# The coupling net's turned products on VectorE alone, in another order, with the last tiles' output rows in the steps of the next attention

## What is computed

```python
def _L0_ffn_ref(x, ...):                       # x: layer-normed rows
    gf = _global_net(x.mean(axis=1, keepdims=True), ...)   # pooled net
    out = x
    for _ in range(3):
        tf = _coupling_net(out, ...)           # 256 -> 256 -> 128 -> 64 -> 1, gelu, sigmoid at the end
        coupling = 0.1 + adaptive_range * (0.7 * gf + 0.3 * tf - 0.5) * 2.0
        out = out + coupling * _twist(out)     # [p_r, -p_i, -o_r, o_i]
    return out
x = x + tanh(g_xattn[0]) * _L0_xattn_ref(layernorm(x), ctx_1024, ...)   # 16 heads of 64
x = x + tanh(g_ffn[0])   * _L0_ffn_ref(layernorm(x), ...)
x = x + tanh(g_xattn[1]) * _L1_xattn_ref(ctx_1024, layernorm(x), ...)   # 16 heads of 16
x = x + tanh(g_ffn[1])   * _L1_ffn_ref(layernorm(x), ...)               # shared expert and top 2 of 8 experts
```

## Time and profile before

| | us |
|---|---|
| median of 3 runs | 711.97 (711.93 to 715.17) |
| the profiled execution, its own time | 712.9 |
| its span, first to last instruction | 711.0 |
| TensorE busy (matmul) | 683.8 |
| VectorE busy | 397.5 |
| ScalarE busy | 287.0 |
| GpSimd busy | 181.0 |
[...]

### The profile page before, as it was taken

One profiled execution on the slowest core, in us unless ns is written; L12 is line 12 of the kernel. 1 busy time (PEld: TensorE's weight loads), 2 busy tenths in 40 slices (PEclk: granted clock), 3 DMA queues, 4 the chain that ended last, 5 costly groups with the idle time before them and its releaser, 6 DMA issues.

```text
span 711.0 us, 11363 instructions
## 1 busy us (share of the span) xinstructions
PE 683.8 (96%) x3640; PEld 475.8 (67%) x3641; DVE 397.5 (56%) x983; ACT 287.0 (40%) x609; POOL 181.0 (25%) x180
## 2 busy tenths in 40 slices
PE   7999999999999987989999999999999999999996
PEld 6777777777754344689999746656545777777765
DVE  4688887788634489478777658222332433333321
ACT  3555533453555653466777541111322222222220
POOL 3100000000002643376000103661123333333433
PEclk9999999999999988699999999999999999999998
DMA  9770000000000006003900201422662656666643
GB/s 291 199 257 16 1 0 0 0 0 0 1 0 8 2 1 222 16 1 128 346 0 1 89 1 38 141 91 80 203 190 56 153 147 179 175 169 164 164 98 36
DMA packets 54934, 65.16 MB, mean 92 GB/s; under 512 B 11582, under 2 KB 37904, under 8 KB 54894
## 3 DMA queue, kind: packets, MB, share of 16 engines
q1 hardware_dynamic: 47806, 55.31, 24.0%
q0 software_dynamic: 7088, 9.35, 7.6%
HBM read 48.48 MB, written 16.00 MB: 91 GB/s over the span
## 4 chain that ended last, share of the span: by engine, by line
PE 87%; issue 3%; DVE 3%; POOL 2%; ACT 2%; DMA 2%; POOLq 0%; SPq 0%; DVEq 0%; ACTq 0%
PE ps L619 78%; PE ps L622 10%; DMA early<-in_wq0T 1%; POOL x_rows L558 0%; POOL x_rows L557 0%; DVE work L2062 0%; POOL rstd L528 0%; ACT early L1479 0%; DVE early L2065 0%; POOL early L554 0%; DMA work<-expert_rows 0%; POOLq L137 0%; ACT work L1340 0%; POOL early L555 0%; ACT middle L1352 0%
## 5 line engine op out<-in xcount | busy, mean ns | idle before, releaser
L619 PE MATMUL ps<-middle,work 128*128 128x256 f32 (+4 forms) x656 | 177.4, 420 | 1.2 <-ACT work L1340 0.8
L1340 ACT ACTIVATE work<-ps 128x512 f32<-128x512 f32 (+3 forms) x209 | 83.0, 437 | 211.2 <-PE ps L622 195.4
L619 PEld LDWEIGHTS ps<-middle,work 128*128 128x128 f32 (+1 forms) x656 | 115.8, 183 | 48.2 <-issue 29.2
L619 PE MATMUL ps<-late,work 32*128 32x154 f32 (+6 forms) x912 | 145.2, 347 | 0.6 <-ACT work L1340 0.6
L585 POOL DMA_INDIRECT out_rows<-masks x47 | 70.4, 1497 | 153.2 <-DMA out_rows<-masks 66.2
L619 PEld LDWEIGHTS ps<-late,work 128*128 128x128 f32 (+3 forms) x912 | 95.3, 184 | 7.9 <-issue 4.7
L619 PE MATMUL ps<-work,late 128*128 128x256 f32 (+2 forms) x424 | 87.9, 367 | 0.6 <-ACT work L1340 0.5
L622 PE MATMUL ps<-consts_sb,work 128*128 128x128 f32 (+1 forms) x564 | 80.5, 277 | 6.1 <-DVE work L1804 3.2
L622 PEld LDWEIGHTS ps<-consts_sb,work 128*128 128x128 f32 (+1 forms) x564 | 65.3, 140 | 26.2 <-issue 11.1
L528 POOL TENSOR_TENSOR rstd<-var_eps,minus_half 128x8 f32<-128x8 f32 (+2 forms) x11 | 14.4, 1311 | 268.7 <-DVE var_eps L1816 268.7
L619 PEld LDWEIGHTS ps<-work,late 128*128 128x128 f32 (+1 forms) x424 | 72.6, 198 | 14.4 <-issue 4.8
(11 more groups left out here) (253 smaller groups left out, 801.7 us busy)
## 6 DMA issues: line engine op xcount, KB each, us to landing
late<-in_w SPq DMA_DIRECT2D x40, 512.0 KB, 4.3
early<-in_w SPq DMA_DIRECT2D x16, 512.0 KB, 10.6
expert_rows<-work SPq DMA_DIRECT2D x36, 130.0 KB, 2.7
work<-expert_rows SPq DMA_DIRECT2D x36, 130.0 KB, 2.2
middle<-in_w SPq DMA_DIRECT2D x8, 512.0 KB, 7.9
out_rows<-x_rows SPq DMA_DIRECT2D x4, 512.0 KB, 3.4
x_rows<-in_x SPq DMA_DIRECT2D x2, 768.0 KB, 10.6
late<-in_ws SPq DMA_DIRECT2D x3, 512.0 KB, 4.0
```

Of the source, the lines that this page charges most:

```text
L619: return nc.tensor.matmul(o, l, r, start=start, stop=stop, **kw)
L1340: return nc.scalar.activation(o, i, ACT.Copy)
```

## The change

- GpSimd loses `turn_z` and `out_rows_`; it keeps only the roots here. The semaphores `f_z1` and `f_row` go.
- VectorE gets `turn_z` of its own (four 512-column operations an item) after `turn_y(0)`, `turn_y(1)` and, for items 2 and 3, after `turn_y(5)`.
- For items 4 to 7 the multiply-add that forms c moves from VectorE to ScalarE: an Identity pass after the tanh in `act4`, behind a wait on that tanh.
- The pooled net's three products move forward, between the halves of `net1("y", 2)`. `to_columns(2)` moves ahead of `net2(1)`, `su1(1)` behind `to_columns(3)`. The order of `net1`, `net2`, `net3` and of their gelus changes, and the banks with it (`PRODUCT_BANK`).
- `couplings_by_row` multiplies by 32 columns of w4 (all alike) where it had one.
- On VectorE `xn0(0, 0)` and `xn0(0, 1)` come before the second pair of rows. The even pairs' rows (8) are spread up to step 1, the odd pairs' rows (8) over the steps 2 to 9, one a step, each with its statistics; `variances(8)` falls into step 6, `variances(9)` and the wait for its root between step 9 and the loop, which now begins at step 10.
- SP's experts' weights wait for `var_done` 10 instead of `f_row` 12.

```diff
-NORMS = [(0, 2), (2, 4), (4, 8), (0, 4), (4, 8), (0, 1), (1, 2), (2, 4), (4, 8), (0, 4), (4, 8)]
+NORMS = [(0, 2), (2, 4), (4, 8), (0, 4), (4, 8), (0, 1), (1, 2), (2, 4), (4, 6), (6, 8), (0, 4), (4, 8)]
+PRODUCT_BANK = {("y", 0): 0, ("y", 1): 4, ("y", 2): 0, ("z", 0): 4, ("y", 3): 0, ("z", 1): 4, ("z", 2): 0, ("z", 3): 4}
...
-            sp.wait_ge(q["f_row"], 12)
-            sp.wait_ge(q["var_done"], 7)
+            sp.wait_ge(q["var_done"], 10)
...
-                        at = 4 * (p // 2) + j
-                        last = mm(ps[:, 4 * k + p % 2, at:at + 1], h3[p][rows, P * j:P * j + P], fw4[rows, 0:1])
+                        at = 32 * (4 * (p // 2) + j)
+                        last = mm(ps[:, 4 * k + p % 2, at:at + 32], h3[p][rows, P * j:P * j + P], fw4[rows, 0:32])
...
             net1("y", 1)
             net2(0)
+            pe.wait_ge(q["f_cp"], evicted("y", 0))
+            to_columns(2, (0, 1))
             pe.wait_ge(q["n_res"], T)
             net2(1)
-            su1(1)
-            pe.wait_ge(q["f_cp"], evicted("y", 0))
-            to_columns(2, (0, 1))
             pe.wait_ge(q["f_cp"], evicted("y", 1))
             to_columns(3, (4, 5))
+            su1(1)
             net3(0)
...
+            net1("y", 2, (0,))
+            pooled([gwt2[:]], [gh1[:]], ps[0:64, 6, 0:B], 1)
+            net1("y", 2, (1,))
+            pooled([gwt3[:]], [gh2[:]], ps[:, 6, 0:B], 2)
+            net4(0)
             net1("z", 0)
-            net4(0)
-            pooled([gwt2[:]], [gh1[:]], ps[0:64, 6, 0:B], 1)
-            net1("z", 1)
-            pooled([gwt3[:]], [gh2[:]], ps[:, 6, 0:B], 2)
-            net1("y", 2)
             net1("y", 3)
             net2(2)
+            net1("z", 1)
             pe.wait_ge(q["f_gact"], 3)
             net2(3)
+            net2(4)
             net1("z", 2)
             net3(1)
-            net2(4)
+            net2(5)
             net4(1)
-            net2(5)
             net1("z", 3)
             net3(2)
             net4(2)
             couplings_by_row(0)
+            net2(6)
             couplings_by_row(1)
-            net2(6)
             net2(7)
             couplings_by_row(2)
             net3(3)
             net2(8)
             net4(3)
             net2(9)
+            net3(4)
             couplings_by_row(3)
-            net3(4)
             couplings_by_row(4)
...
             def act4(n):
 
                 act.wait_ge(q["f_l4"], n + 1)
-                nc.scalar.activation(tt[n], ps[:, 7 - 4 * (n % 2), :], ACT.Tanh, bias=hb[:, 1:2],
-                                     scale=0.5).then_inc(q["f_tanh"], 1)
+                last = nc.scalar.activation(tt[n], ps[:, 7 - 4 * (n % 2), :], ACT.Tanh, bias=hb[:, 1:2], scale=0.5)
+                if n >= NG:
+                    last.then_inc(q["f_t4"], 1)
+                    act.wait_ge(q["f_cpl"], 1)
+                    act.wait_ge(q["f_t4"], n - NG + 1)
+                    last = nc.scalar.activation(tt[n], tt[n], ACT.Identity, bias=cpl[:, 1 + n % 2:2 + n % 2],
+                                                scale=cpl[:, 0:1])
+                last.then_inc(q["f_tanh"], 1)
...
             act1s(8)
-            act1s(9)
             act2(8)
             act4(6)
             act4(7)
+            act1s(9)
             act2(9)
+            act3(4)
             by_row(1, 0, 2)
-            act3(4)
+            by_row(0, 2, 3)
             act1s(10)
-            by_row(0, 2, 3)
             act1s(11)
...
+            def turn_z(n):
+
+                g, c = ffn_group(n), tt[n]
+                seq.sync()
+                at = seq.n
+                for o in range(2):
+                    seq.mark(v.tensor_tensor(dve_u[2 + o], c, ys[:, g, o, :], ALU.mult))
+                for o in range(2):
+                    dve.wait_ge(q["dve_seq"], seq.base + at + o + 1)
+                    seq.mark(v.tensor_tensor(zs[:, g, o, :], zs[:, g, o, :], dve_u[2 + o], ALU.subtract))
...
-            for n in range(6):
+            def out_two(pi, j):
+
+                for k in range(2):
+                    out_row(pi, k, j)
+                seq.sync()
+                for k in range(2):
+                    norm_stats(4 * pi + j + TB * k)
+
+            turn_y(0)
+            turn_z(0)
+            turn_y(1)
+            turn_z(1)
+            for n in range(2, 6):
                 turn_y(n)
+            turn_z(2)
+            turn_z(3)
             two_cycles(0)
             turn_y(6)
             turn_y(7)
...
             xn0(0, 0, "a")
             xn0(0, 1, "a")
+            out_two(0, 1)
+            variances(6)
+            two_cycles(1)
             soft(0, 0, "a")
             dve.wait_ge(q["rstd_done"], 7)
             xn0(0, 2, "a")
+            out_two(0, 2)
             soft(0, 1, "a")
             xn0(0, 3, "a")
+            out_two(0, 3)
+            variances(7)
             three_cycles(1)
...
-            def step1_out(n, a, z):
+            def step1_out(n):
 
                 att1(0, n - 2)
+                if n == 6:
+                    variances(8)
                 soft(0, n, "a")
                 res1(0, n - 2)
+                if n == 6:
+                    dve.wait_ge(q["rstd_done"], 9)
                 xn0(0, n + 2, "a")
-                norm_stats(tile_of(0, n - 2))
-                row_stats(a, z)
...
+                norm_stats(tile_of(n // 2 - 1, n % 2))
+                out_row(1, n % 2, n // 2 - 1)
+                seq.sync()
+                norm_stats(TB // 2 + n // 2 - 1 + TB * (n % 2))
+
+            for n in range(2, 10):
+                step1_out(n)
+            variances(9)
+            dve.wait_ge(q["rstd_done"], 10)
+            with dve.Fori(5, TB - 1) as i:
```

More of the change, by code:

```diff
@@ L207, in build @@
         ys = cut(middle, 0, [NG, 2, G4]); zs = cut(middle, 4096, [NG, 2, G4])
-        dve_u = [cut(work, 1536 + 512 * o, [G4]) for o in range(2)]; pool_u = [cut(work, 2560 + 512 * o, [G4]) for o in range(2)]
-        wz = cut(masks, 1600, [KD, 256]); pool_r = cut(early, 14336, [2, D])
+        dve_u = [cut(work, 1536 + 512 * o, [G4]) for o in range(4)]
+        wz = cut(masks, 1600, [KD, 256])
         turn_t, turn_c = [cut(masks, 2112 + 48 * n, [2, 3, 2, 4]) for n in range(2)]
@@ L818, in to_columns, with net1 @@
                     last.then_inc(q["f_tx"], 1)
-            def net1(kind, n):
+            def net1(kind, n, os=range(2)):
                 g = ffn_group(n)
                 pe.wait_ge(q["f_cp"], max(evicted("x", n), PRODUCT_FREE[kind, n]))
-                for o in range(2):
+                for o in os:
                     for m in range(KD):
-                        last = mm(ps[:, 4 * (n % 2) + o, :], (fw1 if kind == "y" else wz)[:, m, P * o:P * o + P],
+                        last = mm(ps[:, PRODUCT_BANK[kind, n] + o, :], (fw1 if kind == "y" else wz)[:, m, P * o:P * o + P],
                                   st_x[:, m, g, :], m == 0, m == KD - 1)
@@ L1494, in act1, with first @@
                                      bias=par[:, V_CB1 + o:V_CB1 + o + 1]).then_inc(q["f_a1"], 1)
-            def first(n):
-                for o in range(2):
+            def first(n, os=range(2)):
+                for o in os:
                     act1(n, o)
-                    last = copy(ys[:, ffn_group(n), o, :], ps[:, 4 * (n % 2) + o, :])
-                last.then_inc(q["f_cp"], 1)
+                    last = copy(ys[:, ffn_group(n), o, :], ps[:, PRODUCT_BANK["y", n] + o, :])
+                if os[-1] == 1:
+                    last.then_inc(q["f_cp"], 1)
             def second(n):
@@ L1506, in second @@
                     act.wait_ge(q["f_l1"], product("z", n, o))
-                    last = copy(zs[:, ffn_group(n), o, :], ps[:, 4 * (n % 2) + o, :])
+                    last = copy(zs[:, ffn_group(n), o, :], ps[:, PRODUCT_BANK["z", n] + o, :])
                 last.then_inc(q["f_cp"], 1)
@@ L1552, in _ @@
             nc.scalar.activation(gh1[:], ps[:, 6, 0:B], ACT.Gelu, bias=par[:, V_GB1:V_GB1 + 1]).then_inc(q["f_gact"], 1)
-            second(0)
-            act4(0)
-            act4(1)
+            first(2, (0,))
             act.wait_ge(q["f_gmm"], 2)
@@ L1558, in _ @@
                                  bias=par[0:64, V_GB2:V_GB2 + 1]).then_inc(q["f_gact"], 1)
-            second(1)
+            first(2, (1,))
             act.wait_ge(q["f_gmm"], 3)
             nc.scalar.activation(gtan[:], ps[:, 6, 0:B], ACT.Tanh, bias=hb[:, 0:1], scale=0.5).then_inc(q["f_gact"], 1)
-            first(2)
+            act4(0)
+            act4(1)
+            second(0)
             first(3)
             act2(2)
+            act1s(4)
+            second(1)
             act2(3)
-            act1s(4)
+            act1s(5)
             second(2)
-            act1s(5)
             act3(1)
             act2(4)
+            act2(5)
             act4(2)
             act4(3)
-            act2(5)
             second(3)
@@ L2158, in _ @@
             xn0(0, 2, "a")
+            out_two(0, 2)
             soft(0, 1, "a")
```

(18 more changed lines are left out.)

104 lines of the change are left out of this document (17 added, 87 removed).

## The result

The median went from 711.95 to 723.98 us (four runs, 720.23 to 725.24); the ratio is 1.0162, with a 95% interval of 1.0137 to 1.0186. The forecast was 716.3 with an upper end of 720.5: the sign was right, the size was not. The profiled execution of after took 725.24 with a span of 723.4; before it was 712.9 and 711.0.

A forecast was written before the change was run, and what follows sets the result against it. TensorE was taken as the bound, 87% of the chain. First att1 at 303.2, plus 8.75, 49.9, 0.25 and 1.75, put step 10's att1 at 363.9, +4.3 us; added to the 711.97 median: 716.3 us, range 709.0 to 720.5.

The forecast's parts named there:

- Couplings of 32 columns: Row couplings on TensorE, net part: 1.25 us per group of 16 instructions, bounds 1.07 and 1.48.
- Clock at 250 to 257 cured: Wider coupling columns should cure TensorE's clock fall, where eight matmuls had taken 6.73 us instead of 3.6.
- Turned products on VectorE off the path: VectorE's turn_y and turn_z, about 2.5 us each, ready before ScalarE asks: cost 0, cover over 4 us.
- The new wait: TensorE ahead of net2(9): 3.6 us dry until ScalarE's act1s(9), now behind act2(8) and two tanh with passes.
- The clock behind it: Clock fall behind the 3.6 us gap, up to TensorE ready for the second attention: 1.7 us, between 0 and 3.4.
- Rival 3: Slower still: clock down from 262 until the second attention, couplings at 1.48, rows at 1.35: 721 us; chance 0.12.
- R to S 4.8, S to A 15.1: TensorE ready for second attention (R) to first soft (S) 4.8 us; from there to first att1 (A) 15.1.
- Steps 3 to 8 at 7.13, and 0.25 for `variances(8)`: Second-attention steps carrying a row: 7.13 us each, as work behind res1 adds in full; 0.25 for variances(8), bounds 0 and 0.6.
- Rival 1: Steps stay bound by TensorE, rows fall into VectorE's spare time: 6.45 us a step, 710.8 us; chance 0.16.
- Step 2 at 8.75: Second attention's step 2: 6.03 us up to res1 and 2.7 behind it, 8.75 against 8.0 before.
- The exposed root 1.75 us: Between the steps and the loop: variances(9) and the wait for its root add 1.75 us.
- E: The att1 of step 10, after which both kernels have the same instructions: 363.9 against 359.61, +4.3 us.

The follow-up runs named there:

- a2: The changed kernel with four 512-column dummy products filling TensorE's wait between net4(3) and net2(9): 717.04 us, ratio 1.0087 to the kernel before.
- e1: a1 with VectorE's eight rows ahead of res1, two in step 2 and one each in steps 3 to 8, variances(9) in step 9: 706.92 us.
- d1: The changed kernel with the row of steps 2 to 9 ahead of res1, its statistics still behind: 718.82 us, ratio 1.0098 to the kernel before.
- c4: c3 with three more dummy matmuls in step 2, between its scores and its transposes: 701.96 us, ratio 0.9863 to the kernel before.
- c3: The changed kernel with act1s(9) before act2(8), odd pairs' rows on GpSimd, two dummy matmuls each before net2(8) and behind net2(9): 704.14 us.
- a1: The changed kernel with act1s(9) on ScalarE moved back ahead of act2(8): 715.95 us, ratio 1.0056 to the kernel before.
- a5: The changed kernel with the multiply-add of items 4 to 7 back on VectorE instead of ScalarE's added passes: 720.10 us, ratio 1.0107 to before.

## Why the prediction was wrong in size, by its steps

1. *Pooled net*: -0.66 forecast; `act3` started at 245.62, 1.2 us earlier than before. Right, a little short.
2. *Couplings of 32 columns*: 1.25 us a group (1.07 to 1.48) forecast, 0.98 to 1.08 measured. So 32 columns cost here what one did, 1.08 against the 1.07 of the earlier trace rows. Taking the price of a column from a row that mixes shapes was the error. It did not show in the sum: from `act3` to the end of `net3(3)` it took 10.27 us, where 10.26 was forecast, since a wait of 0.65 us for ScalarE that the walk did not have took its place.
3. *Clock at 250 to 257 cured*: right, 1.00 against 0.54.
4. *Turned products on VectorE off the path*: right. Alone it did pairs in 1.29 us, and no TensorE wait at R ended with it.
5. *The new wait*: 3.6 us ended by ScalarE forecast, 4.39 measured. The new pass took 0.81 us, not 0.66, so the two tanh with their passes took 2.98 us and not 2.7, and the first tanh started only as `net4(3)` ended, not 0.4 us before. At full clock the late start behind it costs 3.4 us (a2 against e1).
6. *The clock behind it*: this is the step that failed. I put 1.7 us on it, bounds 0 and 3.4, from the 4 us at 0.57 of the earlier trace rows. It was 7.4 (after against a2): 6.4 behind the new wait, and 1.0 that arose ahead of it, where the clock fell behind the wait of 2.01 us (0.60 at 258 to 262); in the kernel before it had held behind the same wait (1.00 at 261 to 265). The nearest row for a clock behind a wait over 3 us was the other one in the same group: 3.19 us of wait, then 12.4 us at 0.50, of which TensorE worked 11.31 and so lost up to 5.7. I named it as the likeness and then priced from the other. Even that would have been a guess, as 1.4, 5.1 and 6.4 us behind the same wait show; the bound of 3.4 was the error more than the 1.7. Rival 3, the slower one with the clock down to R, was the right mechanism; it had the same wrong price.
7. *R to S 4.8, S to A 15.1*: 3.62 and 14.73 measured. A row was 1.05 us rather than 1.19. These gave back 1.6 us.
8. *Steps 3 to 8 at 7.13, and 0.25 for `variances(8)`*: 7.18 on average, which is the forecast. In these steps what stands behind `res1` adds in full; d1 shows it by taking the row from there (6.52 for 7.11). Rival 1, steps bound by TensorE at 6.45, is refuted for rows in that place, and close (6.52) for rows ahead of `res1`.
9. *Step 2 at 8.75*: 9.29, because the clock was at 0.50 behind TensorE's wait of 3.16 us (308 to 313). What such a clock is worth there c4 shows, 2.2 us (6.34, where c3 has 8.51).
10. *The exposed root 1.75 us*: right as a wait (1.31 on VectorE and the `variances`). But its follow-up was priced at nothing: TensorE dried up for 2.69 us, the clock was at 0.64 in 372 to 376, and step 10 took 1.2 us more. Step 9 itself ran at 0.72 in 360 to 366, 1.9 us more than the 8.9 forecast; a1, a2 and a5 had 9.20 there, so some 1.6 us of it belong to the one execution.
11. *Expert weights later*: cost 0, right. They ran from 371 to about 395 and no wait of the shared expert for them shows.

Against the forecast of E, 363.9, the measured 371.10 is made up of +6.3 at R, -1.6 to A, +0.5 in step 2, nothing in steps 3 to 8 and +1.9 in step 9; behind E come 1.2. Most of this is the clock: 5.7 us at R (7.4 less the 1.7 forecast), and the falls in steps 2, 9 and 10.
